# Third layer's cross attention: turned queries of two heads in three tiles of 128 rows, 256 tokens a unit, scores three heads behind

## The reference

```
q   = rope192( norm(x) @ Wq[h].T @ w_kc_q[h] )          # 1024 tokens x 192, turned by position
q64 = q @ (W_qr[h] @ W_kr[h].T)                         # 192 -> 64, the "narrow" product
key = rope64(ctx)                                        # 64 x 64 a sequence
p   = softmax(q64 @ key.T)                               # 64 x 64 a sequence
out += (p @ key) @ (w_kc_kv[h].T @ Wo[:, h].T)           # 64 -> 256, summed over heads
```

## Time and profile before

| | |
|---|---|
| median of 3 runs | 1648.98 us (1644.61 to 1651.52) |
| profiled execution | 1650.88 us, its span 1649.2 us |
| TensorE (matmul) busy | 1402.5 us, 85% of the span |
| DVE / ACT / GpSimd busy | 833.9 / 531.4 / 276.3 us |
| mean granted TensorE clock | 0.914 |
| `fold_cross` of the third layer | from 920.0 us to about 944 us |
| its `attend`, to the output product | from 945.6 us to 1183.4 us |

### The profile page before, as it was taken

One profiled execution on the slowest core, in us unless ns is written; L12 is line 12 of the kernel. 1 busy time (PEld: TensorE's weight loads), 2 busy tenths in 40 slices (PEclk: granted clock), 3 DMA queues, 4 the chain that ended last, 5 costly groups with the idle time before them and its releaser, 6 DMA issues. The chain is left out here.

```text
span 1649.2 us, 27413 instructions
## 1 busy us (share of the span) xinstructions
PE 1402.5 (85%) x11449; PEld 980.8 (59%) x11449; DVE 833.9 (51%) x1450; ACT 531.4 (32%) x951; POOL 276.3 (17%) x218
## 2 busy tenths in 40 slices
PE   5778986979999977999979889999766578878888
PEld 2447984558867666788657623444655444457545
DVE  4844436552363633433447547666344449981542
ACT  1331223462244643221214311222313423442461
POOL 0133422001120000111100033333001103320200
PEclk8759998988999988999979899999887799999999
DMA  3000002135022000000190600000046300000000
GB/s 98 1 1 4 4 4 70 34 81 115 0 81 93 2 1 29 1 0 1 52 262 2 210 5 1 1 1 1 1 136 200 114 18 1 1 1 0 27 1 26
DMA packets 82907, 69.27 MB, mean 42 GB/s; under 512 B 23352, under 2 KB 80993, under 8 KB 82657
## 3 DMA queue, kind: packets, MB, share of 16 engines
q1 hardware_dynamic: 82016, 65.43, 13.9%
q0 software_dynamic: 768, 2.10, 0.4%
HBM read 55.19 MB, written 12.32 MB: 41 GB/s over the span
## 5 line engine op out<-in xcount | busy, mean ns | idle before, releaser
L1140 PE MATMUL ps<-fixed,work 128*96 128x512 f32 x256 | 118.5, 606 | 8.3 <-DVE fixed L1168 5.4
L1683 PE MATMUL ps<-rounded 128*128 128x512 f32 x384 | 96.3, 408 | 9.4 <-POOL rounded L1706 6.1
L1188 POOL TENSOR_TENSOR weights<-weights,fixed 96x1024 f32<-96x1024 f32 x32 | 75.2, 2349 | 161.9 <-DVE fixed L1168 161.9
L637 PE MATMUL ps<-work,weights 128*128 128x256 f32 x384 | 89.3, 395 | 7.4 <-ACT weights L656 7.4
L1683 PEld LDWEIGHTS ps<-rounded 128*128 128x128 f32 x384 | 74.0, 195 | 29.4 <-issue 9.6
L637 PEld LDWEIGHTS ps<-work,weights 128*128 128x128 f32 x384 | 75.8, 199 | 19.2 <-ACT weights L656 8.1
L1140 PEld LDWEIGHTS ps<-fixed,work 128*96 128x96 f32 x256 | 39.8, 165 | 68.1 <-issue 55.2
L1367 PE MATMUL ps<-work,weights 96*128 96x512 f32 x128 | 64.0, 626 | 14.7 <-DVE work L1390 12.9
L1164 DVE TENSOR_TENSOR weights<-ps,weights 96x1024 f32<-96x1024 f32 x32 | 39.1, 1221 | 72.2 <-PE ps L1140 72.2
L1177 ACT COPY weights<-ps 64x512 f32<-64x512 f32 x32 | 18.6, 580 | 172.8 <-PE ps L1150 172.8
L1706 POOL TENSOR_TENSOR rounded<-weights,rounded 128x256 fp32r<-128x256 f32 x32 | 22.9, 736 | 276.7 <-ACT rounded L1710 276.7
(11 more groups left out here) (441 smaller groups left out, 3018.2 us busy)
## 6 DMA issues: line engine op xcount, KB each, us to landing
weights<-in_L_ffn_masksT SPq DMA_DIRECT2D x32, 256.0 KB, 5.5
sorted_in<-work SPq DMA_DIRECT2D x1, 4992.0 KB, 17.0
work<-sorted_in SPq DMA_DIRECT2D x13, 384.0 KB, 3.9
sorted_out<-work SPq DMA_DIRECT2D x13, 384.0 KB, 2.7
weights<-in_L_ffn_fc_w SPq DMA_DIRECT2D x16, 256.0 KB
weights<-in_L_xattn_Wq SPq DMA_DIRECT2D x2, 2048.0 KB, 10.0
weights<-in_L_xattn_WoT SPq DMA_DIRECT2D x2, 2048.0 KB, 10.3
weights<-in_L_ffn_Wg SPq DMA_DIRECT2D x8, 256.0 KB, 5.7
```

What stands on the lines that cost most here:

```text
L637: last = nc.tensor.matmul(ps[:, (0, 1, 4, 5)[j // 2], (j % 2) * D:(j % 2 + 1) * D], t.ctxT[:, u, j * P:(j + 1) * P], t.pm[:, u, :], start= ...
L1140: last = nc.tensor.matmul(ps[0:96, a, :], qf[:, c, h, 96 * a:96 * a + 96], k.hT[:, c, half * BANK:(half + 1) * BANK], start=c == 0, stop=c ...
L1188: nc.gpsimd.tensor_tensor(ro[:, v % 2, :, :], ro[:, v % 2, :, :], sn, ALU.add).then_inc(s["roped"], 1)
L1683: last = nc.tensor.matmul(ps[:, 2 * (n % 2) + i, :], a[:, q % 2, i, c, :], b[:, c, half * BANK:(half + 1) * BANK], start=c == 0 and part = ...
```

## The change

Heads are taken in pairs. The 192 rows of each of two heads are packed in three tiles of 128 rows: two tiles hold rows 0 to 63 of either half (a) of both heads, and the third holds rows 64 to 95 of both halves of both heads. A unit is a pair of heads and 256 tokens (v = 4u + part), so there are still 32 units. `project` has 6 matmuls of 128x128 by 256 columns in place of 4 of 128x96 by 512; `narrow` has 3 with all 128 rows in place of 2 with 96, and gives both heads at once. DVE's sin product is three instructions in place of one (the third tile is swapped between its two halves of rows), ACT's copies and GpSimd's addition take 256 tokens on 128 rows. The scores wait for all four units of their pair. `scores`, `turn`, `weigh` and what hangs on them come one iteration later (`lag` 3 for 2). In `fold_cross`, `c1` is laid out block-diagonally with zeros (a memset on GpSimd and a wait `czero`), made by twice as many, smaller matmuls and copied by ACT in three parts a bank; `qf` is copied by two instructions a head. The rope table is loaded by 10 DMAs in place of one. `kk`, `ro` and `sn` lie in other places.

```diff
-        for h in range(NH + 5):
+        for h in range(NH + lag + 3):
             if h < NH:
                 q_hooks["pe"](pe, h)
             if h == NH:
                 q_hooks.get("pe_last", none)(pe)
-            if 2 <= h < NH + 2:
-                scores(h - 2)
+            if lag <= h < NH + lag:
+                scores(h - lag)
             if h < NH:
                 q_hooks.get("pe_b", none)(pe, h)
-            if 4 <= h < NH + 4:
-                turn(h - 4)
-            if h >= 6 and h % 2 == 0:
-                weigh((h - 6) // 2)
+            if lag + 2 <= h < NH + lag + 2:
+                turn(h - lag - 2)
+            if h >= lag + 4 and (h - lag) % 2 == 0:
+                weigh((h - lag - 4) // 2)
...
-        eng.dma_start(w.table, d["const_rope192"]).then_inc(sem, 16)
-        n = 32
+        of = d["const_rope192"]
+        for e in range(2):
+            eng.dma_start(w.table[64 * e:64 * e + 64, :, 0:2, :], of[0:64]).then_inc(sem, 16)
+            for half in range(2):
+                rows = slice(64 * half + 32 * e, 64 * half + 32 * e + 32)
+                eng.dma_start(w.table[rows, 0, 2, :], of[64:96, 0, half]).then_inc(sem, 16)
+                eng.dma_start(w.table[rows, 1, 2, :], of[64:96, 1, 1 - half]).then_inc(sem, 16)
+        n = 16 * 11
...
-                for a in range(2):
-                    for i in range(4):
-                        h = 4 * g + i
-                        r = slice(64 * (h % 2), 64 * (h % 2) + 64)
-
-                        last = nc.tensor.matmul(ps[0:96, 5 * (g % 2) + h % 2, (2 * a + i // 2) * DH:(2 * a + i // 2 + 1) * DH],
-                                                w.qr[r, h // 2, a * 96:(a + 1) * 96], w.kr[r, h // 2, :],
-                                                start=True, stop=True, tile_position=(64 * (h % 2), 0))
+                for i in range(4):
+                    p, e = divmod(i, 2)
+                    r = slice(64 * e, 64 * e + 64)
+                    bank = 5 * (g % 2) + e
+                    for rows, width, first, tile in ((64 * e, 64, 0, 0), (64 * e, 64, 96, 1), (32 * e, 32, 64, 2), (64 + 32 * e, 32, 160, 2)):
+                        at = (3 * p + tile) * DH
+                        last = nc.tensor.matmul(ps[rows:rows + width, bank, at:at + DH], w.qr[r, 2 * g + p, first:first + width],
+                                                w.kr[r, 2 * g + p, :], start=True, stop=True, tile_position=(64 * e, rows))
...
+            nc.gpsimd.memset(c1, 0.0).then_inc(s["czero"], 1)
             nc.gpsimd.memset(t.kvt, 0.0).then_inc(s["vzero"], 1)
...
                 for e in range(2):
-                    ins = nc.scalar.copy(cv[:, e], ps[0:96, 5 * (g % 2) + e, 0:256].rearrange("p (a i d) -> p a i d", a=2, i=2))
+                    own = slice(64 * e, 64 * e + 64)
+                    made = ps[:, 5 * (g % 2) + e, 0:384].rearrange("p (n a d) -> p n a d", n=2, a=3)
+                    nc.scalar.copy(c1[own, 2 * g:2 * g + 2, 0:2, own], made[own, :, 0:2, :])
+                    for lower in (32 * e, 64 + 32 * e):
+                        ins = nc.scalar.copy(c1[lower:lower + 32, 2 * g:2 * g + 2, 2, own], made[lower:lower + 32, :, 2, :])
...
-                nc.vector.tensor_copy(qf[:, :, h, :], ps[:, 3 + h % 2, 0:384].rearrange("p (c q) -> p c q", c=2)).then_inc(s["qfs"], 1)
+                e = h % 2
+                made = ps[:, 3 + e, 0:384].rearrange("p (c q) -> p c q", c=2)
+                nc.vector.tensor_copy(qf[:, :, h // 2, 0:2, 64 * e:64 * e + 64], made.rearrange("p c (a q) -> p c a q", a=2)[:, :, :, 0:64])
+                nc.vector.tensor_copy(qf[:, :, h // 2, 2, :].rearrange("p c (a e q) -> p c a e q", a=2, e=2)[:, :, :, e],
+                                      made.rearrange("p c (a q) -> p c a q", a=2)[:, :, :, 64:96]).then_inc(s["qfs"], 1)
...
         def project(pe, v):
-            h, half = divmod(v, 2)
+            u, part = divmod(v, 4)
             if v:
-                pe.wait_ge(s["sined"], v)
-            for a in range(2):
+                pe.wait_ge(s["sined"], 3 * v)
+            for a in range(3):
                 for c in range(KC):
-                    last = nc.tensor.matmul(ps[0:96, a, :], qf[:, c, h, 96 * a:96 * a + 96],
-                                            k.hT[:, c, half * BANK:(half + 1) * BANK], start=c == 0, stop=c == KC - 1)
+                    last = nc.tensor.matmul(seen[:, a, :], qf[:, c, u, a, :], k.hT[:, c, part * D:(part + 1) * D],
+                                            start=c == 0, stop=c == KC - 1)
             last.then_inc(s["q_proj"], 1)
...
-            for a in range(2):
-                last = nc.tensor.matmul(ps[64 * (h % 2):64 * (h % 2) + 64, 2, :], c1[:, a, h, :], ro[:, v % 2, a, :],
-                                        start=a == 0, stop=a == 1, tile_position=(0, 64 * (h % 2)))
+            for a in range(3):
+                last = nc.tensor.matmul(ps[:, 2, 0:D], c1[:, v // 4, a, :], ro[:, v % 2, a, :], start=a == 0, stop=a == 2)
...
-            nc.vector.tensor_tensor(rv, ps[0:96, 0:2, :].rearrange("p a (b t) -> p a b t", t=SEQ),
-                                    bc(w.table[:, 0, :, :], 2, 8), ALU.mult).then_inc(s["cosed"], 1)
+            nc.vector.tensor_tensor(ro[:, v % 2, :, :].rearrange("p a (b t) -> p a b t", t=SEQ),
+                                    seen[:, 0:3, :].rearrange("p a (b t) -> p a b t", t=SEQ),
+                                    bc(w.table[:, 0, :, :], 2, 4), ALU.mult).then_inc(s["cosed"], 1)
             if v:
                 dve.wait_ge(s["roped"], v)
-            nc.vector.tensor_tensor(sn.rearrange("p a (b t) -> p a b t", t=SEQ), swapped,
-                                    bc(w.table[:, 1, :, :], 2, 8), ALU.mult).then_inc(s["sined"], 1)
+            nc.vector.tensor_tensor(sn[:, 0:2, :].rearrange("p a (b t) -> p a b t", t=SEQ), swapped,
+                                    bc(w.table[:, 1, 0:2, :], 2, 4), ALU.mult).then_inc(s["sined"], 1)
+            for half in range(2):
+                there, here = slice(64 - 64 * half, 128 - 64 * half), slice(64 * half, 64 * half + 64)
+                nc.vector.tensor_tensor(by_seq(sn[there, 2, :]), by_seq(seen[here, 2, :]),
+                                        bc(w.table[here, 1, 2, :], 1, 4), ALU.mult).then_inc(s["sined"], 1)
...
-                pool.wait_ge(s["sined"], v + 1)
+                pool.wait_ge(s["sined"], 3 * v + 3)
...
-               1.0, turn_banks=(3, 3))
+               1.0, turn_banks=(3, 3), lag=3)
```

More of the change, by code:

```diff
@@ L569, with attend @@
              "copied", "pv", "ctx", "out", "added", *NORM_SEMS)
-def attend(k, block, s, t, key_rows, q_of, q_hooks, scale, causal=None, turn_banks=(2, 3), turned=True):
+def attend(k, block, s, t, key_rows, q_of, q_hooks, scale, causal=None, turn_banks=(2, 3), turned=True, lag=2):
     nc, ps, x = k.nc, k.ps, k.x
@@ L656, in copy_context @@
                 nc.scalar.copy(dst, src).then_inc(s["ctx"], 1)
-        for h in range(NH + 7):
-            if h >= 7:
-                copy_context((h - 7) // 2, (h - 7) % 2)
+        for h in range(NH + lag + 5):
+            if h >= lag + 5:
+                copy_context((h - lag - 5) // 2, (h - lag - 5) % 2)
             if h < NH:
@@ L665, in _ @@
                 q_hooks.get("act_last", none)(act)
-            if 4 <= h < NH + 4:
-                g = h - 4
+            if lag + 2 <= h < NH + lag + 2:
+                g = h - lag - 2
                 act.wait_ge(s["turned"], g + 1)
@@ L671, in _ @@
                 nc.scalar.copy(t.pT[:, (g // 2) % 2, g % 2, :, :].rearrange("p a b -> p (a b)"), ps[:, turn_banks[g % 2], :]).then_inc(s["copied"], 1)
-            if 2 <= h < NH + 2:
-                g = h - 2
+            if lag <= h < NH + lag:
+                g = h - lag
                 act.wait_ge(s["centred"], g + 1)
@@ L694, in normalise @@
             nc.vector.tensor_tensor(pr, pr, bc(rs, 2, SEQ), ALU.mult).then_inc(s["probs"], 1)
-        for h in range(NH + 2):
+        for h in range(NH + lag):
             if h < NH:
                 q_hooks.get("dve", none)(dve, h)
-            if h < 2:
+            if h < lag:
                 q_hooks.get("dve_b", none)(dve, h)
                 continue
-            g = h - 2
+            g = h - lag
             sc = ps[:, 4 + g % 2, :].rearrange("p (j t) -> p j t", t=SEQ)
@@ L730, in load_latent_cross @@
     if L == "L2_xattn_":
-        w.table = r.take(2, 2, SEQ, rows=96)
+        w.table = r.take(2, 3, SEQ)
     w.wq = r.take(NH, D)
@@ L768, in fold_cross @@
     tmp = spare.take(8, DH)
-    with k.stage("vzero", "vals", "c1", "c1s", "pm", "pms", "qf", "qfs", "rope", "dup", "kkT", "kks") as (block, s):
+    with k.stage("czero", "vzero", "vals", "c1", "c1s", "pm", "pms", "qf", "qfs", "rope", "dup", "kkT", "kks") as (block, s):
         @block.tensor
@@ L1116, in stage_L2_xattn @@
     k.work.clear()
-    qf = k.work.take(KC, NH, 192)
+    qf = k.work.take(KC, NH // 2, 3, P)
     pm = k.work.take(NH // 2, D)
-    kk = k.work.take(TOK)
```

(23 more changed lines are left out.)

15 lines of the change are left out of this document (7 added, 8 removed).

## The result

The changed kernel takes 1622.24 us (median of 4 runs, 1620.76 to 1624.74) against 1650.25 us for the kernel before on the same chip. The ratio is 0.983, with a 95% interval of 0.981 to 0.986. The forecast was 1619 with a range of 1608 to 1633. A second series of the same kernel gave 1625.74 us and 0.987 (0.984 to 0.989).

What follows compares the result with a forecast made beforehand. TensorE's work bound the kernel, the project and DVE round trip only 0.4 us behind. Attend -34.7, tail +0.8 and fold_cross +3.2 made -30.7 against 1650.9, so 1620.2, stated as 1619 us; range 1608 to 1633.

Steps and rivals of the forecast that it cites:

- The bound changes hands: In attend, the round trip of project and DVE, 5.35 us, bounds 27 of 32 units; TensorE bounds five.
- TensorE's part: In attend, project falls from 3.61 to 2.74 us and narrow to 1.43; TensorE's work per unit falls by 1.30.
- DVE's part: In attend, DVE's four instructions per unit take 2.47 us without overlap of the halves, 2.25 if all overlap.
- The sum of `attend`: First project to last narrow takes 178.7 us against 213.4 before, a gain of 34.7.
- GpSimd and L694: In attend, GpSimd's addition takes 1.76 us, ending 0.85 before narrow needs it; L694 ends 0.4 before the next cos.
- The tail: Last narrow to first output product, 24.4 us before, grows by 0.8 us, with ends -0.7 and +4.
- `fold_cross`: The stage before attend grows by 3.2 us, ends +1.5 and +5.5, of which first_products 2.3.
- Loads: Nine more DMAs on SyncE for the rope table, about 0.4 us each, nearly fit before the next DMA and cost nothing.
- The round trip dearer by 0.2 to 0.4: Rival: each project and DVE trip in attend costs that much more, giving 1627 us, 1633 with upper ends elsewhere; chance 0.2.
- the clock: Rival: TensorE's granted clock falls to 1.2 GHz in attend's units without weigh, 1689 us if in all 27; chance 0.03.
- if the clock leaves 1.00 inside the loop: Sign that the prediction is wrong: TensorE's granted clock departs from 1.00 within attend's loop.
- The first rival: The sin halves overlap on DVE in attend, round trip 5.13 us, total 1614.6, or 1613 with cheap first products; chance 0.2.

Runs made afterwards that it cites:

- The split: Changed kernel with DVE's work of a unit split by PSUM bank, project's matmuls waiting for each bank separately: 1607.63 us, ratio 0.975.
- the run without the exchange: Changed kernel with the third tile's two sin halves writing the rows that they read: 1617.95 us, ratio 0.979.
- The version with all repairs: Changed kernel with DVE's work split by bank, alternating first_products, c1's memset in two, scores before narrow: 1596.39 us; larger memset also after DVE's copy: 1596.60.

## Why the prediction was right, step by step

The time lies 3 us above the forecast. That is closer than the terms were: `fold_cross` came out 2.9 us and `attend` 1.0 us dearer, the tail 1.0 us cheaper, and 2.3 us fell away in stretches that the change doesn't touch, which is chance.

**The bound changes hands: right.** Forecast 5.35 us by the round trip, measured 5.41 in 21 units and 5.31 in the four behind a weigh. The split shows it: it lets the trip go and takes 15.1 us out of the loop, 13.4 without the second project's clock, within the 11 to 14 worked out for it. Scores three behind without the packing brought nothing.

**TensorE's part: right.** From start to start project takes 2.70 us for 2.74, narrow 1.30 to 1.39 for 1.43, turn and weigh 2.22 for 2.28.

**DVE's part: right.** The four starts lie 0.87, 0.71 and 0.44 apart, for 0.88, 0.72 and 0.45; the whole is 2.46 for 2.47. The choice between 2.25 and 2.47 rested on one row, L849, and the run without the exchange confirms that rows decide the one step that it changes. The rule of the Trainium skill ("VectorE: DVE Perf Modes", section "Two Vector instructions with no wait between them") names just these starts; the trace agrees. The missing 0.06 of the unit lies between project and cos, 2.90 us for 2.84.

**The sum of `attend`: right, with terms that cancel in part.** 21 units 0.06 too cheap are 1.3 us, and the four behind a weigh 0.2 us the other way. The four with weigh took 6.2 for 6.4, 0.8 us the other way too. The last took 7.4 for 7.2. The lower clock at the start cost 1.7 us where 1.4 was forecast, and in the second project (4.38 us for 2.70), not in the first. 179.6 for 178.7.

**GpSimd and L694: right.** The addition takes 1.81 for 1.76. It covered narrow in the loop. L694's end comes 0.43 to 0.45 us ahead of cos in six of the seven iterations concerned, for 0.4, and 0.15 in one; the cover held.

**The tail: two terms too small that cancel.** One head more was to cost 1.5 us and the clock to give back 0.7; -0.2 was measured for +0.8. The first scores behind the last narrow, in the kernel before and in the changed one:

```profile
1161.49 1.98 PE L592 MATMUL ps<-work,weights 64*64 64x64 f32 x32
...
1131.46 1.15 PE L592 MATMUL ps<-weights 64*64 64x64 f32 x32
```

Before, the last narrow had waited 2.48 us, and at 1158.9 to 1167.4 the granted clock was 0.50 to 0.73: narrow, scores, turn and weigh took 3.2 us more there than the same work elsewhere. In the changed kernel the wait is 0.98 us and the clock stays at 1.00 through that work. So the clock gave back some 3 us and the head cost some 3, by subtraction. That the sum was near is luck. With three behind alone the tail grew by 2.1 us and the loop shrank by 1.9.

**`fold_cross`: the sum's mis-sized term.** "+1.3 to +4.1, I take 2.3" for `first_products` measured +7.1, outside its own ends. A warm group grew by 1.59 us (2.41 for 0.82), where 0.26 to 0.82 was allowed, and the first, at the lower clock, by 2.4. The two rows taken as bounds, the present group and scores, have in common that successive matmuls change rows or columns. The new order keeps four in a row on the same rows, and the order and not the count is the price. The memset cost nothing (0.3 allowed), as the slow products covered it, and the second copies of `qf` 0.2 for 0.6.

That the stretch grew by 6.1 us only, and not 7.3, has a cause that the sum left out. The stage ends when every engine has ended, SyncE too. In the kernel before, SyncE was the last:

```profile
921.38 23.80 SPq L1816 DMA_DIRECT2D weights<-in_L_ffn_masksT  x32
...
942.70 1.42 DVE L857 COPY work<-ps 128x256 f32<-128x256 f32 x4 [0.32 <-PE ps L814]
```

It issued DMAs of the next feed-forward part until 945.18, DVE had ended at 944.12, and the first project came at 945.63; the kernel before with three behind shows the same 0.44 us behind SyncE's last issue. In the changed kernel SyncE ended at 943.79, DVE at 950.04 was the last, and the first project came 0.32 us later. By that 0.32 us the kernel before could have started at 944.4, so by this estimate 1.2 us of longer work in `fold_cross` cost nothing. This is read from the ends in the traces; no run moves the DMAs.

**Loads: right.** The ten table DMAs took 6.6 us of SyncE's queue instead of 1.9, and the loads ended at 839.3 before the next DMA at 843.65.

**The rivals.** The round trip dearer by 0.2 to 0.4 did not come (it was 0.06), and the clock did not fall in the loop as feared: from the third unit on it stayed at 1.00 although TensorE idled up to 1.26 us a unit. It was lower in the second project alone, which taken by the letter is the prediction's sign "if the clock leaves 1.00 inside the loop", at a price of 1.7 us. The first rival, overlapping halves, is excluded by the 0.71 and 0.44.

## What to carry to other kernels

When TensorE's work in a single-buffered loop shrinks, work out the round trip of write and read first: it gives the floor, and releasing one bank earlier than the other can lower that floor at no cost in PSUM. Small matmuls on parts of the array are to be counted in their order, because the same 32 cost 2.41 or 0.98 us. The version with all repairs runs at 1596.4 to 1596.6 us, ratio 0.967 to 0.970, so of the gain that this packing can give some 28 us was taken by the change and 26 to 29 more lay in the waits beside it and in the order of the small matmuls.

## What the runs showed of the hardware

In these traces a copy from SBUF to SBUF on DVE and a memset on GpSimd exclude each other. The copy of 1024 columns took 1.82 us for 0.69 and ended 0.55 after the memset, and the memset behind it 1.49 for 0.95. With the memset moved behind them the two copies of the values took 0.86 us for 2.77. A product of two SBUF tensors beside the same memset kept its 0.69 us. Yet such a product (L694) takes 1.5 to 1.8 us beside GpSimd's addition, and 0.69 in the tail, where GpSimd is idle. The Trainium skill ("SBUF — State Buffer", section "SBUF: two separate sides") describes a lock for the whole instruction, taken by a DVE instruction in a two-port mode, or with two SBUF inputs against a GpSimd instruction that reads; the durations agree in both, though no trace shows in which mode the copy ran.
